# A routed expert layer inside a one-core transformer kernel: earlier shared weights, two shared steps around the last norm, an earlier row table, results gathered ahead

## The reference

```python
gu_s = x2 @ shared_w_gate_up.T                      # 512 -> 2 x 512
g_s, u_s = split(gu_s, 2)
shared_out = silu(g_s) * u_s @ shared_w_down.T      # 512 -> 512
probs = softmax(x2 @ gate_w.T)                      # 16 experts
topk_vals, topk_idx = top_k(probs, 2)               # normalised to sum 1
gu = einsum('th,eih->eti', x2, w_gate_up)           # 16 experts, 512 -> 2 x 128
out_e = einsum('eti,ehi->eth', silu(g) * u, w_down) # 128 -> 512
y = einsum('eth,te->th', out_e, combine) + shared_out
x = x + tanh(g_ffn[2]) * y                          # x2 is layernorm(x)
```

## Time and profile before

| | us |
|---|---|
| three timed runs | 2783.11, 2790.77, 2794.80 (median 2790.77) |
| the profiled execution | 2791.41 |
| its span, first to last instruction | 2789.6 |
| PE busy | 2514.5 (90%) |
| DVE / ACT / POOL busy | 1793.4 / 1266.9 / 1258.3 |

### The profile page before, as it was taken

How to read it: one execution, slowest core, us unless ns; L and a number is a source line. 1 busy time by engine, 2 the same in 40 slices (tenths; PEclk the granted TensorE clock), 3 DMA queues, 4 the chain that set the end, 5 groups by cost and what they waited for, 6 DMA issues and landing times.

```text
span 2789.6 us, 42069 instructions
## 1 busy us (share of the span) xinstructions
PE 2514.5 (90%) x13734; PEld 2105.8 (75%) x13734; DVE 1793.4 (64%) x3360; ACT 1266.9 (45%) x3698; POOL 1258.3 (45%) x1407
## 2 busy tenths in 40 slices
PE   4899999998889999999988887778679999999979
PEld 3788888887678888888767776655468888888854
DVE  4777777767677777777656665442257777777662
ACT  2455455454245555555425444123235555555421
POOL 4545445454144444444326555144345444444343
PEclk7999999999999999999998998789889999999989
DMA  3111111111012222111100001149511111110054
GB/s 118 49 31 35 39 35 31 37 36 38 5 38 99 78 96 97 54 39 51 42 8 12 8 9 35 46 128 321 193 39 46 40 39 35 35 35 27 5 193 173
DMA packets 66539, 172.63 MB, mean 62 GB/s; under 512 B 10227, under 2 KB 10929, under 8 KB 63898
## 3 DMA queue, kind: packets, MB, share of 16 engines
q1 hardware_dynamic: 50080, 112.49, 12.5%
q0 software_dynamic: 13040, 54.58, 5.9%
q10 hardware_dynamic: 3210, 2.89, 0.4%
HBM read 153.65 MB, written 33.16 MB: 67 GB/s over the span
## 4 chain that ended last, share of the span: by engine, by line
PE 76%; DVE 7%; DMA 5%; issue 5%; POOL 4%; ACT 3%; ACTq 0%; SPq 0%; POOLq 0%; DVEq 0%
PE B_qkv L695 29%; PE B_out L695 19%; PE B_oT L766 4%; PE B_s L746 4%; PE B_qT L736 3%; PE B_pt L756 3%; PE B_oT L695 2%; PE B_s L747 1%; PE B_s L695 1%; PE B_oT L833 1%; DMA raw<-slots_y,tables 1%; POOL ring_l L1930 1%; PE B_qT L927 1%; PE B_out L1010 1%; PE B_pt L820 1%
## 5 line engine op out<-in xcount | busy, mean ns | idle before, releaser
L1193 ACT ACTIVATE W<-S,nmx 128x128 f32<-128x128 f32 x768 | 298.0, 395 | 50.7 <-DVE nmx L1455 47.3
L1938 POOL TENSOR_SCALAR rn<-ss 128x5 f32<-128x5 f32 x128 | 25.5, 199 | 628.5 <-DVE ss L1398 628.5
L1090 ACT ACTIVATE sq<-B_qkv 128x640 f32<-128x640 f32 x128 | 90.4, 707 | 428.8 <-PE B_qkv L695 428.8
L1959 POOL TENSOR_TENSOR S<-S,mask 128x512 f32<-128x512 f32 x192 | 251.0, 1308 | 20.0 <-ACT S L1031 18.8
L1473 DVE SCALAR_TENSOR_TENSOR X<-B_out,gates,X 128x512 f32<-128x512 f32 x200 | 150.2, 751 | 168.0 <-PE B_out L695 165.0
L1998 POOL TENSOR_TENSOR W<-W,rden 128x512 f32<-128x512 f32 x192 | 200.5, 1044 | 87.1 <-DVE rden L1460 87.0
L695 PE MATMUL B_out<-ring_h,oT_h 128*128 128x512 f32 x516 | 208.2, 404 | 16.4 <-DVE kT L1445 12.2
L695 PE MATMUL B_qkv<-ring_h,xnT_h 128*128 128x512 f32 x512 | 216.5, 423 | 4.9 <-DVE xnT_l L1311 4.9
L746 PE MATMUL B_s<-kT,qT_h 128*128 128x256 f32 x768 | 203.5, 342 | 9.5 <-DVE xnT_l L1311 8.5
L695 PE MATMUL B_out<-ring_l,oT_h 128*128 128x512 f32 x516 | 207.1, 401 | 0.0
L695 PE MATMUL B_out<-ring_h,oT_l 128*128 128x512 f32 x516 | 206.8, 401 | 0.0
(11 more groups left out here) (459 smaller groups left out, 8033.9 us busy)
## 6 DMA issues: line engine op xcount, KB each, us to landing
raw<-in_pieces SPq DMA_DIRECT2D x270, 256.0 KB
slots_x<-in_zero SPq DMA_DIRECT2D x16, 1030.0 KB
w<-in_experts SPq DMA_DIRECT2D x8, 1024.0 KB, 11.6
slots_y<-S SPq DMA_DIRECT2D x31, 256.0 KB
X<-in_x ACTq DMA_DIRECT2D x8, 256.0 KB, 3.3
raw<-in_ctxT SPq DMA_DIRECT2D x8, 256.0 KB
rows_x<-xn SPq DMA_DIRECT2D x8, 256.0 KB, 2.1
raw<-in_quant SPq DMA_DIRECT2D x4, 256.0 KB
```

Of the source, the lines that this page charges most:

```text
L1193: t = act.activation(W[:, k, cols(r)], S[:, k, cols(r)], ACT.Exp, bias=nmx[:, k, r:r + 1], accum_out=den[:, k, r:r + 1])
L1959: pool.tensor_tensor(S3, S3, m.unsqueeze(1).to_broadcast([P, R, P]), ALU.add).then_inc(*masked.now((layer, u)))
```

## The change

```diff
+LANDING2 = 1.1
@@ small_heads
-        self.at(first + CHUNKS - 1, 92, "hold", None)
+        self.at(first + 2 * R * (NB - 1) - 4, 92, "hold", None)
@@ ffn2
-            i, row = first + 2 * e, base + 3 * (e // 2)
+            i, row = first + 2 * e - 2, base + 3 * (e // 2)
-            self.at(first + n, 74, "up", n, ...)
-            self.at(first + n + 1, 75, "down", n, ...)
-        self.at(first, 70, "fill_dispatch2")
+            at = ((first - 6, 30), (first - 3, 62))[n] if n < 2 else (first + n - 2, 74)
+            self.at(*at, "up", n, ...)
+            at = (first + n - 1, 75) if n else (first - 2, 75)
+            self.at(*at, "down", n, ...)
+        self.at(first - 6, 31, "hold", self.weights2[1][1])
+        self.at(first - 2, 61, "hold", None)
+        self.at(first - 5, 2, "fill_dispatch2")
-        self.at(first + 3, 70, "rank2")
-        self.at(first + 3, 71, "table2")
-        self.at(first + 4, 70, "scatter2")
-        self.at(first + 8, 80, "turn_ids2")
-        first += len(self.steps2) + 1
+        self.at(first + 2, 78, "rank2")
+        self.at(first + 2, 79, "table2")
+        self.at(first + 3, 70, "scatter2")
+        self.at(first + 5, 70, "load_ids2")
+        self.at(first + len(self.steps2) - 2, 80, "turn_ids2")
+        first += len(self.steps2) - 1
-            self.at(first - 4 if t < 4 else first + t - 2, 10, "fetch_weights2", t)
+            self.at(first - 3 if t < 4 else first + t - 2, 10, "fetch_weights2", t)
+            self.at(first + max(0, b - 2), 1, "gather2", b)
             self.at(first + b, 40, "collect2", b)
@@ split_next
+        first = self.first.get(2, now)
+        landing = LANDING2 if now is not None and first < now < first + CHUNKS else LANDING
@@ build
-        collected2 = (...)[:, 0:2 * TOP2 * D].rearrange("p (k n) -> p k n", n=D)
+        collected2 = (...).rearrange("p (k n) -> p k n", n=D)
-        up_banks = [((B_qkv[:, 0:D], "qkv"), (B_qkv[:, D:2 * D], "qkv")), ((B_qT, "qT"), (B_kT, "kT"))]
+        up_banks = [((B_qT, "qT"), (B_kT, "kT")), ((B_qkv[:, 0:D], "qkv"), (B_qkv[:, D:2 * D], "qkv"))]
+        places2 = 12
@@ vector_program, collect2
+                dve.wait_ge(*rope_in[b].of((2, TOP2 - 1)))
                 for k in range(TOP2):
-                    place = 2 * (b % 2) + k
-                    dve.wait_ge(*rope_in[place].of((2, b)))
-                    add_to_x(b, collected2[:, place, :], per_row2[7 + k][:, b:b + 1], ("ffn2", b, k))
+                    add_to_x(b, collected2[:, (TOP2 * b + k) % places2, :], per_row2[7 + k][:, b:b + 1], ("ffn2", b, k))
@@ pool_program: collect2 becomes gather2
-                    place = 2 * (b % 2) + k
-                    if b > 1:
-                        pool.wait_ge(*x_add.of(("ffn2", b - 2, k)))
+                    place = TOP2 * b + k
+                    if place >= places2:
+                        pool.wait_ge(*x_add.of(("ffn2", (place - places2) // TOP2, k)))
@@ sync_program: the load of turn_ids2 becomes load_ids2; fill_dispatch3
-                for place in range(2 * TOP2):
-                    sync.wait_ge(*rope_in[place].of((2, NB - 2 + place // TOP2)))
+                sync.wait_ge(*x_add.of(("ffn2", NB - 1, TOP2 - 1)))
```

More of the change, by code:

```diff
@@ L224, in ffn2 @@
             up, down = self.weights2[e // 2][e % 2], self.weights2[e // 2][2]
-            self.at(first + n, 74, "up", n, needs=[up], frees=[(up, "gate_up", (n, 1), first + n + 0.7)] if half else ())
-            self.at(first + n + 1, 75, "down", n, needs=[down],
-                    frees=[(down, "down", (n, NB // 2 - 1), first + n + 1.7)] if half and e % 2 else ())
-        self.at(first, 70, "fill_dispatch2")
+            at = ((first - 6, 30), (first - 3, 62))[n] if n < 2 else (first + n - 2, 74)
+            self.at(*at, "up", n, needs=[up], frees=[(up, "gate_up", (n, 1), at[0] + 0.7)] if half else ())
+            at = (first + n - 1, 75) if n else (first - 2, 75)
+            self.at(*at, "down", n, needs=[down],
+                    frees=[(down, "down", (n, NB // 2 - 1), at[0] + 0.7)] if half and e % 2 else ())
+        self.at(first - 6, 31, "hold", self.weights2[1][1])
+        self.at(first - 2, 61, "hold", None)
+        self.at(first - 5, 2, "fill_dispatch2")
         for part in range(5):
             self.at(first + part // 2, 76 + part % 2, "choose2", part)
-        self.at(first + 3, 70, "rank2")
-        self.at(first + 3, 71, "table2")
-        self.at(first + 4, 70, "scatter2")
-        self.at(first + 8, 80, "turn_ids2")
-        first += len(self.steps2) + 1
+        self.at(first + 2, 78, "rank2")
[4 more added lines that the diff above has]
+        first += len(self.steps2) - 1
         for t in range(TILES2):
-            self.at(first - 4 if t < 4 else first + t - 2, 10, "fetch_weights2", t)
+            self.at(first - 3 if t < 4 else first + t - 2, 10, "fetch_weights2", t)
             self.at(first + max(0, t - 2), 11, "fetch_rows2", t)
@@ L334, in split_next @@
         item = self.landing[0]
-        if now is not None and item["when"] is not None and now - item["when"] < LANDING:
+        first = self.first.get(2, now)
+        landing = LANDING2 if now is not None and first < now < first + CHUNKS else LANDING
+        if now is not None and item["when"] is not None and now - item["when"] < landing:
             return
@@ L2037, in collect2 @@
                 for k in range(TOP2):
-                    place = 2 * (b % 2) + k
-                    if b > 1:
-                        pool.wait_ge(*x_add.of(("ffn2", b - 2, k)))
-                    pool.indirect_dma_start(out=collected2[:, place, :], out_offset=None, in_=slots_y,
+                    place = TOP2 * b + k
+                    if place >= places2:
+                        pool.wait_ge(*x_add.of(("ffn2", (place - places2) // TOP2, k)))
+                    pool.indirect_dma_start(out=collected2[:, place % places2, :], out_offset=None, in_=slots_y,
                                             in_offset=bass.IndirectOffsetOnAxis(ap=slot2_i[k][:, b:b + 1], axis=0)
-                                            ).then_inc(*rope_in[place].now((2, b)))
+                                            ).then_inc(*rope_in[b].now((2, k)))
             def scatter3(b):
@@ L2153, in fill_dispatch2, with load_ids2 @@
                 sync.dma_start(dispatch[:, 0:DISPATCH2], io["dispatch2"]).then_inc(*consts2_in[1].now(0))
-            def turn_ids2():
+            def load_ids2():
                 sync.wait_ge(*scattered[0].of(("ids", TOP2 - 1, NB - 1)))
```

8 lines of the change are left out of this document (4 added, 4 removed).

## The result

The changed kernel takes 2762.86 us (median of five runs, 2759.98 to 2769.25) where the kernel before, beside it on the chip, takes 2791.90 (2783.11 to 2795.80). The ratio is 0.9901, with a 95% interval of 0.9878 to 0.9924: 29 us or 1% faster, against 2759 forecast. On another chip the same kernel, timed once more, has a ratio of 0.9918 (0.9903 to 0.9934), 23 us. The profiled execution took 2759.98 us, the fastest of the five, of which the span is 2758.2; its granted clock is 0.961. From span to span the difference is 31.4.

What follows compares the result with a forecast made beforehand. TensorE lacks work behind the last chunk and as the next attention begins; transfers bound the tiles between. Row-table cast -20.9 (including +3 for splits), tiles 0, gathers -11: -31.9 from 2791.41, 2759.5, by the median 2759; range 2744 to 2780.

Steps and rivals of the forecast that it cites:

- Splits in the chunks: Last chunks: six weight-half splits moved there cost +3 us, between 0 (all in gaps) and 8.
- Behind the last chunk: After the last chunk: copy of the last transposes about 8.4 us sooner, norm of block 6 and router about 2 more.
- The two steps: Around the last norm: `up(0)` 8 us, `up(1)` 5.45, `down(0)` before the router; router ends at 1767.5, norm gains only 3.3.
- To the scatters: From router to first scatter: `rank2` 1.6 us sooner, first scatter at 1803.6, 7.9 us sooner.
- The row table: Scatters to the table's cast: TensorE ends last after a 10 us stall, cast at 1839.4 against 1860.29, -20.9 us.
- Tiles: The 31 expert tiles: bound by transfers, length unchanged at 130 us, so 0.
- Gathers: Next attention's beginning: results gathered ahead remove DVE waits, -11 us, between 0 and -24.
- the 2 us for the clock: Next attention's beginning: 2 us of the gathered-ahead gain, for a clock that is up sooner.
- The clock did come back: Rival, next attention: clock rises 35 us sooner as gaps shrink, 11 us more gain, 2748 us; chance 0.17.
- The gathers did give: Rival denied here: gathering ahead in the next attention gives nothing, only the first part stays, 2770.5 us; chance 0.13.
- the splits cost nothing: Rival denied here: late loads make splits cost the chunks 10.4 us instead of 3, 2767 us; chance 0.12.
- the stall did not spread over the steps: Rival denied here: stall follows scatters into shared steps, 10 us each; cast 39 later, 2819 us, slower; chance 0.04.

Runs made afterwards that it cites:

- the splits alone: Kernel before with only six splits of the shared weights moved into the last chunks, 1.1 places between load and split: 2782.48 us, ratio 0.9976.
- The pause: Changed kernel with POOL waiting, behind the twelfth of its sixteen scatters, until ACT has done the last shared step's tanh: 2766.98 us, ratio 0.9926.
- The gathers alone: Kernel before with only the last part of the change, results gathered ahead: 2779.85 us, ratio 0.9963.

## Why the prediction was right

*Splits in the chunks.* +3 was taken, -0.4 to +1.2 measured in the traces with 1.1 places. The end at 0 of the bounds was the right one: in the changed kernel's trace no copy waits for a transfer by more than 0.86 us, in the others by at most 1.94.

*Behind the last chunk.* -10.4 was taken, -10.5 measured by the splits alone.

*The two steps.* Here the prediction was off. It gave `up(0)` 8 us, since the clock there had been 0.61. But the half clock was read in a stretch in which TensorE was busy for 10.75 of 22 us. With the splits gone and `up(0)` in their place it is busy for 8.89 of 9 us, at full clock (1.00, 2.4 GHz) from 1734, and `up(0)` puts 3.8 us on the path though it is 5.48 long. `out2(7)` came at -6.7 instead of -1.1. A clock read in a stretch was used for work in that stretch without its gaps. The Trainium skill (TensorE: Matmul & The Clock Gate, HAM oscillation) has it that closing such waits keeps the array warm; behind the last chunk the trace agrees, 0.61 to 1.00, in the next attention it hardly does, 0.78 to 0.81. The norm itself gave -1.5 instead of -2.2: `ln_apply` and the four additions lie ahead of the router as forecast.

*To the scatters.* -3.6 at the slot numbers, so 4.5 were lost again between router and slots. Forecast were 1.7. Most of the difference is the clock again, now the other way: the first bank of `up(2)` takes 4.88 us in the chain above, where the prediction had 2.7. The granted clock from 1758 to 1763 is 0.56, after a stretch (1752 to 1758) in which TensorE was busy for 3.43 of 6 us. Then TensorE waits 4.01 us for the last `choose2`, where 3.3 were forecast. The 5.8 us between the last slot number and the first scatter fell to 0.3, as forecast. By luck these errors nearly cancel: `out2(7)` 5.6 us sooner than forecast, the router 4.8, the slot numbers 2.0, and -9.1 at the first scatter, where -7.9 was forecast.

*The row table.* -18.4 against -20.9. The prediction let TensorE end last, after a stall of 10 us, then put 2.7 us of additions and the cast, and had the table 2.3 us ahead of that. This sum met the cast within 2.5 us, but the wait that it names is not the one that ends last. POOL's run of 20 issues took 25.9 us, as forecast, and the table's load went out 2.2 us behind it, as forecast. What was left out is the split of a weight half that DVE has to do ahead of the last four additions, and whose load can only go out behind that run: 13.5 us from the run's end to the cast, where the prediction's places have 9.9. TensorE and ACT end just ahead of that, so a nearly right number came from the neighbouring path. The pause shows it: with TensorE 12 us sooner the cast came no sooner.

Nor is code loading what ended ACT's stall in the trace. It records instruction packets (queue, kind: packets, MB, share of 16 engines); in the changed kernel the last one before it is in the microsecond from 1801, the next in that from 1835, and none is recorded between, though ACT goes on at 1826.40. In the trace of before they lie in the microseconds from 1822 and from 1856, and DVE goes on at 1833.10. The rows of the two packets in the changed kernel:

```profile
q14 instruction: 1, 0.01, 13.8%
```

```profile
q14 instruction: 1, 0.01, 6.7%
```

The Trainium skill (Runtime: NRT & Kernel Launch, Instruction fetch mechanics) says that crossing a block of code is mostly hidden. No run here speaks against that; the packets and the pause say that the stall set against it had another cause.

*Tiles.* 133.4 us before and 134.5 after, from the first turn to the first gather; nine traces in which nothing near the tiles was changed have 133.4 to 136.7. A zero within the scatter.

*Gathers.* -11 forecast, -11.5 between the traces (91.2 to 79.8). The root behind eight issues stands 10.3 us behind the first gather instead of 6.5, as forecast; with four of them behind the root 3.5 us come back. How the rest divides over the single units, and whether the 2 us for the clock were there, no run shows.

*Rivals.* The clock did come back behind the last chunk, but not in the next attention, where it went from 0.78 to 0.81; 2748 was not reached. The gathers did give; the splits cost nothing; the stall did not spread over the steps.

*Parts by time.* The gathers alone give 10 us (0.9963) and the splits alone 7 (0.9976); the whole gives 28 (0.9901) and in its second timing 23 (0.9918). What is left, 6 to 11 us, is for the shared steps and the table's load. No run takes the shared steps alone.

## What to carry to other kernels

When an edit takes gaps away, price what follows at the clock that it will have without them, not at the clock read in the old trace. Look at what stands in the queue of the issuing engine behind a long run of indirect issues: here a single split, 1.3 us of work, held a load, and by it the row table's cast, until the run was over. A stall that catches the eye need not be the one that sets the end; ACT's 14.5 us could be taken away without gain as long as that second way stayed. And count from a place ahead of the change before explaining a few microseconds.

## What the runs showed of the hardware

In the ten traces with the changed order of steps and no pause, ACT stood still for 9.6 to 16.1 us while POOL issued: 16 scatters, 1.26 us from one to the next in the median and 1.30 to 1.36 on average, and in seven of the ten 4 gathers behind them. ACT went on 1.3 to 3.4 us after POOL's run of issues had ended, whether with a scatter or a gather, in all fourteen traces. In the three with the old order it had also done one instruction within the run, behind 7.3 to 10.1 us of idle time (in before at 1833.82, with the run ending at 1837.22), so the hold is not complete. Nor does it begin with the run: in the changed kernel's trace ACT worked until 1811.9, eleven issues in, and behind the pause eight issues held nobody up. Of the 14.52 us in that trace ACT waited 1.7 for PE's gate half; 12.8 it stood still with its inputs there. The DMA share was 0.02 in the scatters' last 8 us (1811 to 1819), so transfers did not crowd it out. In that time DVE lost 0.75 and 1.41 us in single gaps, and TensorE, a little later, 1.02 and 1.01 between single matmuls. What ACT waits for is not named in any trace; that it is held by POOL's issuing is shown by the pause, a single trace; how, and why only after some ten issues, is open.

The first row gather, of 128 rows, was used 3.5 us after its issue when nothing stood ahead of it, and 8.5 us after it behind four weight gathers of the same queue.
